# TensorE's branch over the large-bound path, written between named blocks and with a branch prefetch hint

## What is computed

```python
x = x + 0.5 * ffn(layernorm(x))
x = x + attn(layernorm(x))          # 16 heads of 8; every 4th key and the keys within 8 places
x = x + 0.5 * ffn(layernorm(x))

# attn
q = q * sigmoid(unity_scale)
scores = einsum('bhqd,bhkd->bhqk', q, k) / sqrt(D)
scores = where(allowed, scores, -inf)      # allowed: j % 4 == 0 or |i - j| <= 8
attn = softmax(scores)
out = einsum('bhqk,bhkd->bhqd', attn, v) ... @ o_w + o_b

# ffn
h = butterfly(layernormed @ W_exp + b_exp, up_weights)
h = gelu(h + up_bias)
y = butterfly(h, down_weights) @ W_con + b_con + down_bias
```

## Time and profile before

| | us |
|---|---|
| median of three runs | 289.7 (289.55 to 293.16) |
| the profiled execution | 286.8 |
| its span, first to last instruction | 285.0 |
| around the span | 1.8 |
| TensorE busy in the span | 250.8 (88%) |
| ScalarE busy in the span | 197.6 (69%) |
| VectorE busy in the span | 129.5 (45%) |

### The profile page before, as it was taken

How to read it: one execution, slowest core, us unless ns; L and a number is a source line. 1 busy time by engine, 2 the same in 40 slices (tenths; PEclk the granted TensorE clock), 3 DMA queues, 4 the chain that set the end, 5 groups by cost and what they waited for, 6 DMA issues and landing times.

```text
span 285.0 us, 6954 instructions
## 1 busy us (share of the span) xinstructions
PE 250.8 (88%) x2919; PEld 135.9 (48%) x2919; DVE 129.5 (45%) x426; ACT 197.6 (69%) x254; POOL 7.3 (3%) x12
## 2 busy tenths in 40 slices
PE   2598888989736999989999989999899999889985
PEld 0465474847401444435444435434345444476654
DVE  5985649696584111323453135154225321445310
ACT  1754438383635999987899987999887999634430
POOL 9100000000000000000000000000000000000000
PEclk9999999999975999999999999999999999999999
DMA  7930000576789133113113311321230000001111
GB/s 222 242 98 4 0 0 1 175 205 179 150 273 322 59 80 80 48 35 78 52 33 80 80 45 37 80 73 24 66 80 2 0 3 2 2 0 39 38 37 37
DMA packets 23873, 21.85 MB, mean 77 GB/s; under 512 B 4727, under 2 KB 22071, under 8 KB 23819
## 3 DMA queue, kind: packets, MB, share of 16 engines
q1 hardware_dynamic: 22726, 21.02, 27.1%
q10 hardware_dynamic: 1112, 0.34, 0.5%
HBM read 13.98 MB, written 7.56 MB: 76 GB/s over the span
## 4 chain that ended last, share of the span: by engine, by line
PE 79%; DVE 10%; ACT 4%; issue 4%; DMA 1%; DVEq 0%; ACTq 0%
PE ps L634 22%; PE ps L612 21%; PE ps L476 11%; PE ps L435 8%; PE ps L644 3%; PE ps L619 3%; DVE xnorm L876 2%; PE ps L449 2%; PE ps L664 2%; ACT probs_all L822 1%; PE ps L652 1%; PE ps L461 1%; DVE stats L850 1%; PE ps L422 1%; DVE ctx_t L1082 1%
## 5 line engine op out<-in xcount | busy, mean ns | idle before, releaser
L818 ACT ACTIVATE probs_all<-ps 128x1024 f32<-128x1024 f32 x128 | 123.1, 1022 | 20.4 <-PE ps L612 13.8
L612 PE MATMUL ps<-q_slots,k_strided 75*128 75x512 bf16 x250 | 65.8, 386 | 3.7 <-ACT probs_all L822 2.5
L634 PE MATMUL ps<-probs_all,v_strided 128*32 128x256 f32 x1024 | 69.0, 388 | 0.0
L634 PEld LDWEIGHTS ps<-probs_all,v_strided 128*32 128x32 f32 x1024 | 27.3, 110 | 32.5 <-issue 12.3
L612 PEld LDWEIGHTS ps<-q_slots,k_strided 75*128 75x128 bf16 x250 | 20.6, 98 | 38.6 <-issue 13.2
L1069 DVE RECIPROCAL rden<-ps 128x16 f32<-128x16 f32 x16 | 4.1, 258 | 71.0 <-PE ps L652 71.0
L729 ACT ACTIVATE gelu_h<-ps,bias_up 128x512 f32<-128x512 f32 x32 | 21.9, 687 | 19.8 <-PE ps L435 19.7
L476 PE MATMUL ps<-down_folded,gelu_h 128*128 128x128 f32 x256 | 30.5, 277 | 2.3 <-ACT gelu_h L729 2.3
L476 PEld LDWEIGHTS ps<-down_folded,gelu_h 128*128 128x128 f32 x256 | 29.2, 192 | 4.9 <-ACT gelu_h L729 2.8
L435 PE MATMUL ps<-xnorm_t,up_folded 128*128 128x512 f32 x64 | 29.3, 600 | 1.7 <-ACT xnorm_t L720 1.0
L1095 DVE SCALAR_TENSOR_TENSOR probs_all<-probs_all,mask_k_sb 128x1024 f32<-128x1024 f32 x16 | 19.6, 1224 | 9.4 <-ACT probs_all L822 8.9
(11 more groups left out here) (108 smaller groups left out, 205.8 us busy)
## 6 DMA issues: line engine op xcount, KB each, us to landing
q_slots<-q_parts SPq DMA_DIRECT2D x16, 288.0 KB
k_local<-k_local_parts SPq DMA_DIRECT2D x48, 78.0 KB
q_parts<-prologue_or_parts SPq DMA_DIRECT2D x9, 384.0 KB, 3.6
k_strided<-k_strided_parts SPq DMA_DIRECT2D x12, 96.0 KB
q_parts<-last_parts SPq DMA_DIRECT2D x3, 384.0 KB, 4.3
out<-resid SPq DMA_DIRECT2D x4, 256.0 KB, 2.3
k_local_parts<-prologue_or_parts SPq DMA_DIRECT2D x3, 288.0 KB, 4.3
resid<-L_attn_x SPq DMA_DIRECT2D x1, 768.0 KB, 10.0
```

What stands on the lines that cost most here:

```text
L612: mm = pe.matmul(PS[:, b0 + i, :], KS[:, ch, G * g + h, :], QS[:, g, h, :], start=True, stop=True)
L634: mm = pe.matmul(PS[VC * h:VC * (h + 1), 6 + n % 2, 0:QB // 2], VS[:, ch, at:at + VC], probs, start=(ch == 0 and r == 0), stop=False, skip ...
L818: act.activation(PE_[:, ch // 2, 2 * m:2 * m + 2, ch % 2, :], PS[:, b0:b0 + 2, :], ACT.Exp).then_inc(p_ready, 1)
```

## The change

TensorE's `If` ... `end_ifs` becomes a conditional branch between two named blocks. The block `pe_large_bound` holds the same instructions as the body of the `If` did, and ends with a branch to `pe_bounded`, where the rest of the stream stands. The branch carries a hint whose place is marked in the loop's last round, ahead of `keep_clock(0, 2)`. Nothing is changed on the other engines: VectorE and SP keep their `If`.

```diff
                 if b == NB:
+                    skip_hint = pe.mark_branch_hint_location()
                     keep_clock(0, 2)
...
             pe.wait_ge(flag_set, 1)
-            with pe.If(pe.value_load(FLAG[0:1, 0:1], min_val=0, max_val=1) == 0):
+            pe.br_cond(pe.value_load(FLAG[0:1, 0:1], min_val=0, max_val=1) == 0, "pe_large_bound", "pe_bounded").branch_hint(skip_hint)
+            with nc.body("pe_large_bound", valid_engines=[pe.engine]):
                 for b in range(NB):
                     pe.wait_ge(ld_ks[b], 16 * PARTS)
...
                 for k, h in ((0, 0), (0, 1), (1, 0), (1, 1), (2, 0)):
                     first_score(k, h)
-            pe.end_ifs()
+                pe.br("pe_bounded")
+            nc.switch_bb("pe_bounded")
             first_score(2, 1).then_inc(s_ps, 3)
```

## The result

| | before | after |
|---|---|---|
| median of 20 runs, us | 289.62 (286.85 to 293.45) | 285.22 (283.17 to 289.17) |
| ratio, 95% interval | | 0.988 (0.9848 to 0.9911) |
| profiled execution, us | 286.8 | 284.14 |
| its span, us | 285.0 | 282.3 |
| mean granted clock in it | 0.98 | 0.988 |

The medians lie 4.4 us apart, where 4.4 were forecast; the ratio, which leaves out on either side the runs over 1.5% above the fastest, stands for 3.5 us (2.6 to 4.4). So the change is real and smaller than 2%. The two profiled executions are only 2.7 us apart, and the trace says why.

What follows compares the result with a forecast made beforehand. TensorE, 88% busy, was taken to bound the kernel, standing still at its branch. The 4.40 us saved there less 0.05 for the split's signal gave 4.35, say 4.4: 289.7 to 285.3 us, range 283.9 to 290.0.

Steps and rivals of the forecast that it cites:

- What bounded, and what the long branch was: TensorE sets the end from the attention on; its 4.472 us branch waits for the target's code, fetched only when decided.
- The branch costs what it costs where no code is missing: Term at TensorE's branch: with the target's code there, it falls from 4.472 us to about 0.07, so 4.40 us go.
- What the hint costs: Term for one added sequencer instruction on TensorE: 0.1 us, hidden behind keep_clock, where TensorE waits for VectorE's xnorm anyway.
- None between 82.0 and 86: Sign on TensorE's code queue q8: a packet lands between 70 and 82 us, none between 82.0 and 86.
- Under 0.2: Sign on TensorE's sequencer: the compare-and-branch falls from 4.472 us to under 0.2.
- The sixth exponential meets the last split: On ScalarE, 4.40 us earlier it starts at 88.82, when VectorE's last split ends; the wait costs some 0.05 us.
- With the same lag the clock is back: TensorE's clock, after falling to half, returns at 88.24 us, ahead of the second group of values at 88.48.
- the case in which the clock comes back late: Rival: TensorE's clock returns no earlier than before, at 92.64 us; gain only 2.5 us, 287.2 us; chance 0.06.
- The rival "no effect": Hinted code is lost at the packet border before TensorE's branch, or the hint names the fall-through; 289.7 us, chance 0.18.
- The rival on the slower side: Hinted packet displaces the one TensorE enters next, stalling it about 4.4 us near 72.3 us; 294.1 us, chance 0.05.

## Why the prediction was right, and where it was off

- **What bounded, and what the long branch was: right.** The 4.47 us were the fetch of the target's code. With the hint the packet came earlier, one packet fewer came in all, and without the hint but with the blocks the time was back.
- **"The branch costs what it costs where no code is missing", 0.07 us: mis-sized.** With the code on board it took 0.41 to 0.50 us on TensorE in every kernel with a working hint, and 0.08 to 0.09 not taken. The 0.07 came from VectorE, whose path is much shorter: 108 instructions more when it is run (534 for 426). The term is 3.97 us, not 4.40. That the gap ahead of the product still shrank by 4.43 was luck: the register load happened to be 0.46 us shorter. Whether the 0.4 us belong to the jump into another packet wasn't tried.
- **What the hint costs: right.** 0.055 us, hidden: TensorE still waited 0.61 us for xnorm behind `keep_clock`.
- **The signs.** "None between 82.0 and 86" failed to the letter: a packet landed between 85 and 86 us. It isn't the target's, since the branch had ended at 83.0. "Under 0.2" for the branch failed with the term above.
- **The sixth exponential meets the last split: right.** It started 8.28 us after the flag; 12.59 less 4.35 is 8.24. It came 0.08 us behind the split's end at 89.77 us, for which I had estimated 0.05.
- **"With the same lag the clock is back": failed.** The clock fell 2.8 us after the flag, where it was 1.8 before, and came back 5.55 us after TensorE had begun to work without a break, not 3.27, which is the lag of the earlier trace rows (89.37 to 92.64 us). So the second group of values still ran at half, and unit 2 began 0.8 us later than forecast in the profiled execution (3.59 gained for 4.35). The lag is no constant: it was 3.27 and 5.55 us here, and with the blocks alone 14.98 (from 90.75 to 105.73 us, whole stretch at half 20.48). I had taken one row for a rule. The gain of 3.59 us lies about midway between the forecast's course and the case in which the clock comes back late (2.5 us, given 0.06).
- **The median nevertheless came out, at 285.2 for 285.3: in part luck.** Two steps were off, and the ratio of the result puts the gain at 3.5 us, with 4.4 at the edge of its interval. A part that the sum doesn't have lies in the clock, and this part is argued, not shown. The clock fell in every run of either kernel whose clock is on record, but less after the change: the mean clock of a run was 0.965 to 0.98 before (23 runs timed beside the experiments) and 0.968 to 0.994 after (20 runs). The runs with a lower mean clock are the longer ones: before, 286.8 to 289.1 us at 0.98 and 291.4 to 293.9 at 0.965. The shorter branch probably takes away part of that as well, which would make up for the branch term that was too large.
- **The rival "no effect": its mechanism is refuted.** I let the border between hint and branch speak against the hint; it is the very thing that the hint needs. The hints at 41.8 and 69.6 us, ahead of the border whose fetch comes at 76 us, worked, those at 78.0 and 80.3 us didn't. No loss came of it, and if the packet counts are read rightly (one between 270 and 340 us with the hint, two without), a packet was still on TensorE after five others had come. How many packets TensorE keeps no run shows; the 0.18 for this rival was my estimate of how easily the hinted one is lost.
- **The rival on the slower side** went wrong at its first step. The hinted packet did take the place of the next straight one, but not of one that the way through the program needs: behind the branch it isn't wanted. Even with the branch not taken, the straight packet came in time, though there TensorE stood waiting for loads until 110 us; a path without such a wait wasn't tried.

## What to carry to other kernels

If an engine's compare-and-branch lasts some microseconds and a packet of its code queue lies inside, look for a jump beyond the code on board: here a hint took 4.0 of the 4.5 us away. In this case it had to stand ahead of the last packet border before the branch, some 255 instructions being a packet (4337 in 17): at 69.6 us it worked, 28 us further ahead as well, and behind the border, at 78.0 and 80.3 us, it was worth nothing. Then look at the clock before asking for more. Idle stretches of 1 to 2 us around the branch were followed here by 3.4 to 17 us at half clock, and by 10 to 20 us where the branch was long and nothing filled the wait; products that nobody reads, put into the hole, gave about as much as the branch itself (2.8 us beside 3.0), and together with the hint took the spread out of the runs (0.6 us for 6). A range of 6 us between runs of one kernel is worth a look at each run's mean clock.

## What the runs showed that was not expected

- The branch hint, as I read the packets, acted at a packet border, not when it was executed: at 41.8 us it was as good as at 69.6 us (a branch of 0.497 and 0.502 us), at 78.0 and 80.3 us it did nothing for a branch at 82 to 83 us (5.02 and 4.58 us). It replaced the straight fetch there (24 packets for 25 with the branch taken).
- The same branch with a fetch on demand took 4.23 to 5.04 us in five kernels.
- The taken branch with a working hint took 0.41 to 0.50 us on TensorE, against 0.083 and 0.093 us not taken, and 0.072 and 0.055 us taken on VectorE and SP.
- Two idle stretches of TensorE, 1.6 and 1.2 us with one product between them, went with 6.83 us at half clock after the change and 17.07 us with the hint two borders ahead; putting a product into one of them kept the full clock in one of eight runs, into both in all five.
- The same register load of the flag took 0.49 to 1.14 us from kernel to kernel.
